# Recurrent layers in blocks of 8 tokens: pair products and block states in place of a scan over all 512 tokens

## The reference

```python
def step(s, rkvw):
    r_t, k_t, v_t, w_t = rkvw
    a = k_t[..., :, None] * v_t[..., None, :]
    out = jnp.einsum('bhi,bhij->bhj', r_t, u * a + s)
    s = a + w_t[..., :, None] * s
    return (s, out)
_, out = jax.lax.scan(step, s0, rkvw)
# then: each head's 16 outputs normalised (mean, variance), * gn_w + gn_b, * g
x1 = x + og * g @ Wo.T
```

## Time and profile before

| | us |
|---|---|
| median of 3 timed runs | 4790.81 (4787.45 to 4797.15) |
| the profiled execution, its own time | 4800.18 |
| its span in the profile | 4798.4 |
| PE busy in the span | 3797.2 (79%) |
| DVE busy in the span | 3378.0 (70%) |
| POOL busy in the span | 2302.9 (48%) |
| ACT busy in the span | 2119.3 (44%) |

### The profile page before, as it was taken

How to read it: one execution, slowest core, us unless ns; L and a number is a source line. 1 busy time by engine, 2 the same in 40 slices (tenths; PEclk the granted TensorE clock), 3 DMA queues, 4 the chain that set the end, 5 groups by cost and what they waited for, 6 DMA issues and landing times. The chain is left out here.

```text
span 4798.4 us, 50379 instructions
## 1 busy us (share of the span) xinstructions
PE 3797.2 (79%) x15616; PEld 2145.1 (45%) x15616; DVE 3378.0 (70%) x5559; ACT 2119.3 (44%) x4624; POOL 2302.9 (48%) x2245
## 2 busy tenths in 40 slices
PE   7888976867888897686788889768668888877766
PEld 4455732424545573252454546234245454623424
DVE  5677379697667738969665773896966577388696
ACT  5576422413657732231365773223137477322313
POOL 4544455354454545535345454543534544454363
PEclk9999977888999998788899999878889999987888
DMA  3123111101212311110121221011022122201102
GB/s 124 39 80 88 53 44 44 44 27 70 70 42 75 88 53 44 49 39 27 70 70 46 74 85 61 36 53 35 27 76 67 49 75 80 77 20 53 35 27 79
DMA packets 95226, 275.38 MB, mean 57 GB/s; under 512 B 25936, under 2 KB 26704, under 8 KB 73808
## 3 DMA queue, kind: packets, MB, share of 16 engines
q1 hardware_dynamic: 94928, 271.84, 17.7%
HBM read 201.49 MB, written 4.19 MB: 43 GB/s over the span
## 5 line engine op out<-in xcount | busy, mean ns | idle before, releaser
L1282 POOL TENSOR_TENSOR prod<-state,rT 128x512 f32<-128x512 f32 x512 | 698.2, 1367 | 662.1 <-DVE state L1060 605.3
L775 POOL TENSOR_SCALAR probs<-probs,row_inv 128x512 f32<-128x512 f32 x1024 | 693.7, 694 | 639.5 <-DVE row_inv L690 639.5
L1060 DVE TENSOR_TENSOR_SCAN state<-decay,s,kvp 128x512 f32<-128x512 f32 x512 | 911.6, 1782 | 12.7 <-POOL prod L1282 12.7
L634 ACT ACTIVATE probs<-probs,row_max 128x512 f32<-128x512 f32 x1024 | 733.3, 725 | 131.2 <-DVE row_max L706 130.0
L529 PE MATMUL ps<-ident,probs 128*128 128x128 f32 x4096 | 605.4, 289 | 172.2 <-ACT pT L628 145.6
L529 PEld LDWEIGHTS ps<-ident,probs 128*128 128x128 f32 x4096 | 476.7, 146 | 382.5 <-ACT pT L628 209.6
L339 PE MATMUL ps<-mix,wring 128*128 128x512 f32 x1024 | 591.6, 677 | 4.8 <-DMA wring<-in_blocks_dram 4.8
L1197 ACT ACTIVATE state<-s 128x1 f32<-128x1 f32 x512 | 102.0, 202 | 1062.2 <-POOL prod L1282 1062.2
L906 PE MATMUL ps<-vstack,pick 128*128 128x512 f32 x512 | 373.7, 732 | 177.0 <-DVE kvp L1052 177.0
L628 ACT ACTIVATE pT<-ps 128x512 f32<-128x512 f32 x768 | 429.8, 603 | 107.8 <-PE ps L529 107.2
L504 PE MATMUL ps<-kstack,qstack 96*128 96x512 f32 (+1 forms) x1024 | 381.6, 467 | 16.8 <-DMA qstack<-hi 7.0
(11 more groups left out here) (142 smaller groups left out, 6526.2 us busy)
## 6 DMA issues: line engine op xcount, KB each, us to landing
wring<-in_blocks_dram SPq DMA_DIRECT2D x151, 1024.0 KB, 5.0
qstack<-hi SPq DMA_DIRECT2D x256, 64.0 KB, 2.0
kstack<-hi SPq DMA_DIRECT2D x256, 64.0 KB, 2.0
maskA<-in_mask_dram SPq DMA_DIRECT2D x9, 1024.0 KB, 7.5
rows<-in_rows_dram SPq DMA_DIRECT2D x8, 1024.0 KB, 4.5
qstack<-hi SPq DMA_DIRECT2D x256, 32.0 KB, 2.0
qstack<-lo SPq DMA_DIRECT2D x128, 64.0 KB, 2.0
kstack<-lo SPq DMA_DIRECT2D x128, 64.0 KB, 2.0
```

The lines of the kernel that those rows point to most:

```text
L634: nc.scalar.activation(p, p, ACT.Exp, bias=row_max[:, n % PSLOTS, qc:qc + 1], scale=-1.0, accum_out=row_sum[:, n % PSLOTS, qc:qc + 1]).the ...
L775: nc.gpsimd.tensor_scalar(p, p, row_inv[:, (n - 1) % PSLOTS, qc:qc + 1], 1.0, ALU.mult, ALU.mult)\
L1060: nc.vector.tensor_tensor_scan(state[:, u % 3, 1:L + 1], decay[:, ug, :], kvp[:, u % 3, :], s0[:, ug, uj:uj + 1], ALU.mult, ALU.add)\
L1282: nc.gpsimd.tensor_tensor(prod[:, t % PRODS, :], state[:, t % 3, 0:L], rT[:, hg % 2, :], ALU.mult)\
```

## The change

The recurrence over 512 tokens is replaced by blocks of 8. What a token receives from tokens of its own block is built from products of pairs, doubled in distance: same token (`rk0`, with u), 1 apart (`rk1`), then the second half of 4 from its first half (`rk2`) and the second half of 8 from its first (`rk4`); k and r are multiplied in place by the decays that lie between. `pair_sums` sums each product per head on PE, DVE multiplies by v (`bonus`), and PE adds it, centred per head, into bank 7 (`bonus_low`, `bonus_high`). What comes from earlier blocks goes through states: `fresh_state` multiplies each block's keys by its values (64 matmuls on 32 x 32 tiles of the array), DVE runs 16 scans over the 64 blocks (`states`), the states are spread to block-diagonal form, four heads by ACT and four by DVE (`spread`), and `from_state` multiplies them by r (2 x 32 matmuls on 128 x 32 tiles). The result is turned into bank 7 (`tokens_to_y`). The variance per head is a matmul with `head_mean`, and POOL raises all 128 x 512 values to -0.5 (`inverse_root`). Wo runs chunk by chunk of features, two chunks of it ahead of the last variance. In each head group the keys are turned to token-major (`keys_to_tokens`) ahead of the next group's key projection (`middle(hg, 0)`).

The diff, cut to its core:

```diff
+            def values_to_tokens(hg):
...
+                for tc in range(C):
+                    m = nc.tensor.matmul(tile[:, tc * P:(tc + 1) * P], vT[:, hg % 2, tc * P:(tc + 1) * P], centre[:, :],
...
+            def pair_sums(hg, level):
...
+                bank, src = ((0, rk0[:, :]), (1, rk1[:, :]), (2, rk2[:, :, :, :]))[level]
+                nc.tensor.matmul(ps[:, bank, 0:256 if level == 1 else 512], head_sum[:, :], src, start=True, stop=True)\
...
+            def pair_sums4(hg):
...
+                for part in range(2):
+                    nc.tensor.matmul(take(pe, 'sums4', l, hg, part), head_sum[:, :], rk4[:, 2 * part:2 * part + 2, :, :],
+                                     start=True, stop=True).then_inc(*tile_ready.reach('sums4', l, hg, part))
...
+            def bonus_low(hg):
...
+                nc.tensor.matmul(y_bank, centre[:, :], rk0[:, :], start=True, stop=False, skip_group_check=True)
+                nc.tensor.matmul(y_bank.rearrange('p (b two) -> p b two', two=2)[:, :, 1], centre[:, :], rk1[:, :],
+                                 start=False, stop=False, skip_group_check=True)
...
+            def bonus_high(hg):
...
+                    m = nc.tensor.matmul(by8[:, :, 1, :], centre[:, :], rk4[:, s, :, :], start=False, stop=False,
...
+            def keys_to_tokens(hg):
...
+                    m = nc.tensor.transpose(tile[:, tc * P:(tc + 1) * P], kT[:, hg % 2, tc * P:(tc + 1) * P], ident[:, :])
...
+            def fresh_state(hg):
...
+                for tc in range(C):
+                    for r in range(4):
+                        rows_ = slice(32 * r, 32 * r + 32)
+                        for q in range(4):
+                            out = ps[32 * q:32 * q + 32, r, :].rearrange('p (two t x) -> p two t x', two=2, t=C)[:, :, tc, :]
+                            m = nc.tensor.matmul(out, k_tok[rows_, tc, 32 * q:32 * q + 32],
+                                                 v_blocks[rows_, tc, q, :, :, :].rearrange('p two b j -> p two (b j)'),
+                                                 start=True, stop=True)
...
+            def from_state(hg, half, tile):
...
+                for tc in (2 * half, 2 * half + 1):
+                    for b4 in range(4):
+                        for q in range(4):
+                            g32 = 4 * tc + q
+                            m = nc.tensor.matmul(tile[32 * q:32 * q + 32, tc * P:(tc + 1) * P],
+                                                 r_blocks[:, 512 * b4 + 32 * g32:512 * b4 + 32 * g32 + 32],
+                                                 state_bd[:, 4 * g32 + b4 - NB // 2 * half, :],
+                                                 start=(b4 == 0), stop=(b4 == 3), skip_group_check=True)
...
-            def reduce(group):
...
-            def centring(c):
-
-                pe.wait_ge(*act_done.when('rec', l, c))
...
-            for t in range(C * HS + lag):
...
-                    nc.tensor.matmul(ps[:, t % 4, :], pick[:, jh * P:(jh + 1) * P], vstack[:, hg % 2, half, :],
-                                     start=True, stop=True)\
...
-            centring(C - 1)
-
-            def wait(pe, c, t):
-                if c == 0:
-                    pe.wait_ge(*dve_done.when('gn', l, t))
-            pe_turn(pe, l, centred, 'gnT', wait)
...
+                    m = nc.tensor.matmul(y_bank[:, tc * P:(tc + 1) * P], y_tok[:, tc, :], ident[:, :], start=False,
...
+                nc.tensor.matmul(take(pe, 'var', l, hg), head_mean[:, :], sqT[:, :], start=True, stop=True)\
...
+            def middle(hg, n):
+                if hg + 1 < C:
+                    project(hg + 1, 'krv'[n])
+                else:
+                    gate(n)
+
+            for hg in range(C):
+                values_to_tokens(hg)
+                pair_sums(hg, 0)
+                pair_sums(hg, 1)
+                if hg > 0:
+                    tokens_to_y(hg - 1)
+                pair_sums(hg, 2)
+                keys_to_tokens(hg)
+                middle(hg, 0)
+                if hg > 0:
+                    variance(hg - 1)
+                fresh_state(hg)
+                pair_sums4(hg)
+                bonus_low(hg)
+                middle(hg, 1)
+                bonus_high(hg)
+                tile = from_state(hg, 0, None)
+                middle(hg, 2)
+                from_state(hg, 1, tile)
+            wo(0)
+            tokens_to_y(C - 1)
+            wo(1)
+            variance(C - 1)
+            gate(C - 1)
+            wo(2)
+            wo(3)
...
+            def pair_products(hg):
...
+                nc.vector.scalar_tensor_tensor(rk0[:, :], r, col(f'u_{l}', hg), k, ALU.mult, ALU.mult)\
...
+                times(rk1[:, :], r1[:, :, 1, 0], k1[:, :, 0, 0], 'rk', l, hg, 1)
...
+                times(k1[:, :, 0, 0], k1[:, :, 0, 0], w[:, :, 1, 0], 'k2', l, hg)
+                times(r1[:, :, 1, 0], r1[:, :, 1, 0], w[:, :, 0, 0], 'r2', l, hg)
...
+                times(rk2[:, :, :, :], r2[:, :, 1, :].unsqueeze(1).to_broadcast(wide),
+                      k2[:, :, 0, :].rearrange('p b s -> p s b').unsqueeze(3).to_broadcast(wide), 'rk', l, hg, 2)
...
+                times(rk4[:, :, :, :], r4[:, :, 1, :].unsqueeze(1).to_broadcast(wide),
+                      k4[:, :, 0, :].rearrange('p b s -> p s b').unsqueeze(3).to_broadcast(wide), 'rk', l, hg, 4)
...
+                times(k4[:, :, 0, :], k4[:, :, 0, :], w[:, :, 1].unsqueeze(2).to_broadcast(wide), 'k8', l, hg)
...
+                times(in_blocks(4), r.rearrange('p (g b t) -> p b g t', b=4, t=8)[:, :, :, 4:8],
...
+                    nc.vector.tensor_tensor(rk4[:, two, :, :], i0, i1, ALU.mult)\
...
+                    ins = nc.vector.scalar_tensor_tensor(
+                        fresh[:, 16 * tc:16 * tc + 16, :].rearrange('p (r b) j -> p r (b j)', r=4), ps[:, 0:4, cut],
+                        masks[:, 12:13], other[:, :, cut], ALU.mult, ALU.add)
...
+                for j in range(HS):
+                    ins = nc.vector.tensor_tensor_scan(entry[:, 1:NB, j], w8[:, hg, 0:NB - 1], fresh[:, 0:NB - 1, j],
+                                                       s0c[:, hg, j:j + 1], ALU.mult, ALU.add)
...
+            def spread(hg, half):
...
+                for h in range(HEADS // 2, HEADS):
+                    ins = nc.vector.tensor_scalar(state_bd[:, :, HS * h:HS * (h + 1)],
+                                                  entry[:, NB // 2 * half:NB // 2 * (half + 1), :], masks[:, 4 + h:5 + h], None,
+                                                  ALU.mult)
...
+            def variance_out(hg):
+                dve.wait_ge(*tile_ready.when('var', l, hg))
+                nc.vector.tensor_scalar(rstdT[:, :], ps[:, ring.bank('var', l, hg), :], 1e-5, None, ALU.add)\
...
+            def normalise(hg):
+                dve.wait_ge(*pool_done.when('rstdT', l, hg))
+                nc.vector.scalar_tensor_tensor(yn[:, hg, :], yT[:, :], col(f'gn_w_{l}', hg), rstdT[:, :], ALU.mult, ALU.mult)\
...
-            for t in range(n + 1):
...
-                    nc.vector.tensor_tensor(kvp[:, t % 3, :], kT[:, hg % 2, :], ps[:, t % 4, :], ALU.mult)\
...
-                    nc.vector.tensor_tensor_scan(state[:, u % 3, 1:L + 1], decay[:, ug, :], kvp[:, u % 3, :],
...
+            for hg in range(C):
+                pair_products(hg)
+                for level in range(3):
+                    bonus(hg, level)
+                if hg > 0:
+                    variance_out(hg - 1)
+                bonus(hg, 4)
+                states(hg)
+                spread(hg, 0)
+                if hg > 0:
+                    normalise(hg - 1)
+                if hg == C - 1:
+                    gated(0)
+                spread(hg, 1)
...
+            low_part('gated', 0, 2)
+            gated(1)
+            gated(2)
+            low_part('gated', 1, 2)
+            low_part('gated', 2, 2)
+            variance_out(C - 1)
+            normalise(C - 1)
+            gated(C - 1)
+            low_part('gated', C - 1, 2)
...
+                nc.scalar.activation(y_tok[:, :, :], ps[:, ring.bank('yt', l, hg), :], ACT.Copy)\
...
+                nc.scalar.activation(sqT[:, :], ps[:, OBANK, :], ACT.Square).then_inc(*act_done.reach('sqT', l, hg))
+                nc.scalar.activation(yT[:, :], ps[:, OBANK, :], ACT.Copy).then_inc(*act_done.reach('yT', l, hg))
...
+                for b4 in range(4):
+                    out = v_blocks[:, :, :, :, b4, :].rearrange('p t q two j -> p (t q two) j')
+                    ins = nc.scalar.activation(out, ps[:, ring.bank('vt', l, hg), :].rearrange('p (x j) -> p x j', j=HS),
+                                               ACT.Identity, scale=masks[:, b4:b4 + 1])
...
+            for hg in range(C):
+                if hg > 0:
+                    y_tokens(hg - 1)
+                value_blocks(hg)
...
+                nc.scalar.activation(in_blocks(0), rT[:, hg % 2, :].rearrange('p (g b t) -> p b g t', b=4, t=8)[:, :, :, 0:4],
...
+                if hg > 0:
```

(39 more changed lines are left out.)

516 lines of the change are left out of this document (265 added, 251 removed).

## The result

| | median of the runs | ratio to before |
|---|---|---|
| before | 4793.98 us (4787.45 to 4810.35, 4 runs) | 1 |
| changed | 6794.94 us (6789.43 to 6797.91, 4 runs) | 1.4165, 95% interval 1.4128 to 1.4203 |
| forecast | 4555 us, range 4400 to 4880 | 0.950 |

A forecast was written before the change was run, and what follows sets the result against it. DVE was taken to bound the recurrent passes before, PE after. Groups 133 plus tail 35.6 make 168.6 us against 198 a pass; eight passes save 235 from 4800.2, giving 4565, timed median 4555; range 4400 to 4880.

The forecast's parts named there:

- What bounds the kernel before: Recurrent scans: DVE decides, busy 158.13 of 160 us, against PE's 110.14.
- I take 8 us, six times the product, as an estimate: Tail of a pass: POOL raises 512 values to -0.5 in 8 us.
- The bounds of 1.4 and 100 us: POOL's power of 512 values: 1.4 us if like a product, 100 us at 0.2 us an element.
- the right rival: POOL's power (p us) is long: slower than before beyond p = 15.1 us, 4950 us at p = 20; chance 0.15.
- That rival's formula: Long power keeping DVE out: excess over 7.6 us counts in three groups, over 8 in the tail; 4p - 31.
- The group, 32.7 us: One head group: PE's 28.1 us at clock 0.9 gives 31.2, with 1.5 of waits 32.7.
- The small tiles: Small matmuls on PE: four run side by side, 0.0275 us an instruction, 7.0 us a group.
- the rival of tiles alone: All small matmuls run one by one at 0.11 us: 21.2 us more a group, 5310 us; chance 0.05.
- `from_state`, which uses all rows, would go one by one: Middle-way rival on PE: only these 128 instructions run alone, 14.1 us for 3.5, kernel 4930 us; chance 0.05.
- The scan of 63 at 0.33: DVE's sixteen scans of 63 elements in a group: 0.33 us each, 5.3 together.
- The lock of 4.5 us: Tail: POOL's weight split after `inverse_root` and a DVE instruction keep each other out, adding 4.5 us.
- The keys' order "at nothing": Turn of keys ahead of the projection, which hides ACT's copy: costs nothing; without that cover 0.8 us a group.

The follow-up runs named there:

- e2_half: Changed kernel with POOL's power on half of the columns and a product on the other half, whose root is left out: 5509.92 us.
- e1_product: Changed kernel with POOL's power replaced by a product of the same operands, the root left out: 4475.85 us.
- g3_alone: Changed kernel with ScalarE square root and VectorE reciprocal for the power, plus `fresh_state` reordered to use each array square four times running: 4812.54 us.
- h1_first_behind: Changed kernel with ScalarE square root, VectorE reciprocal and weight splits in quarters, plus keys turned behind the projection in group 0 alone: 4425.78 us.

## Why the prediction was wrong, point by point

**What bounds the kernel before**: right. DVE's 158 of 160 us did go, and without the power the kernel is 7% faster.

**The step that failed is the tail's term "I take 8 us, six times the product, as an estimate"** for POOL's power of 512 values. It is 82.15 us. The bounds of 1.4 and 100 us held it, and their upper end had been worked out from the only row of the same kind, by 0.2 us an element; e2_half shows 0.16. I chose near the row of the same size and another operation. The two bounds lay a factor of 70 apart (1.4 and 100) and the break-even at 15.1, yet my chance for a power beyond it was about 0.1, and the range ended at 4880, where p is about 18. The text named the right rival, gave its price and its point of decision, and then did not believe it.

**That rival's formula** (what is over 7.6 us counts in three groups, what is over 8 in the tail) gives at 82.15 us 297.8 a pass more, 4555 + 8 x 297.8 = 6937; measured 6795. The waits measured 71.3, 71.3, 71.3 and 82.25. So some 11 us were hidden in a group, not 7.6. Its condition that the power keeps DVE out failed: the scans' median is 0.326 us beside the power and 0.325 without it (e1_product). For the time that decided little: had the scans and the first spreads (5.7 us on DVE) stood behind the power too, it would have cost up to that much in each of 24 groups, some 136 us beside the 2001, an estimate.

**The group, 32.7 us**: 29.2 measured wherever the power is gone. PE's sum of 28.1 at full clock was 27.38 (small tiles 5.8 in place of 7.0, as the sixteen squares of `fresh_state` overlap: 1.9 for its 128), and the clock was 1.00 where I took 0.9, which alone is 3.1 us. The wait of PE for the spread was 1.8, forecast 1 to 1.5. That PE ends last in a group was right.

**The small tiles**: the earlier trace rows were the right guide, and the rival of tiles alone fell; g3_alone comes about half of the way to it by another loop order, 0.060 us each at full clock where the rival had 0.11. That `from_state`, which uses all rows, would go one by one fell too: 64 in 1.95 us, 0.03 each, near the 0.0275 that had four of them side by side.

**The scan of 63 at 0.33**: 0.326 in duration, but 0.25 from start to start. A spread was set at 0.565 and stands at 0.42. So DVE is busy 18.5 us a group, forecast 21.2.

**The lock of 4.5 us**: right in the tail (4.97 beside the split). Missed was the first split, which meets DVE in the last group (4.98 at 988.94). It was not in the sum: in e1_product PE waits 3.41 us there, against 1.82 in the group before. From the power's end to the last normalised tile it was 17.8 us, forecast 4.5 + 2.8 + 1.0 + 8.9 = 17.2.

**The keys' order "at nothing"**: wrong in group 0, where the turn waits for DVE with the projection behind it; h1_first_behind puts 12 us on that for the whole kernel. The 0.8 us without the cover was 0.83.

With 1.3 us for the power the sum of the prediction would have been 4555 - 8 x 6.7 = 4501, against 4476 for e1_product: all other errors together come to 25 us, that of the one term to about 2300. That the 25 is so small is in part luck, since errors cancel in it. The two passes of sample 0 take 154.3 and 156.5 us there (first product to last normalised tile), against 168.6 - 6.7 = 161.9, which alone is some 50 us over eight passes. The tail is as forecast, 29.0 against 28.9; the groups were set too long. If the other samples are alike, the rest lies outside the passes, where the forecast put nothing; no run places it.

## What to carry to other kernels

Where the trace of before has no row for an operation at its new size, the row of the same operation at another size bounds it better than the row of another operation at the same size; and a term with bounds that far apart, on the path, decides the forecast and deserves the chance that its bounds give it. A long instruction off the busiest engine becomes the bound of everything queued behind its reader; ask what stands behind that reader before asking what it hides. Cut long GpSimd instructions with two inputs into pieces where VectorE has short ones to run beside them, and let small tiles of TensorE's array take turns over its squares: a repeated square costs its own time and, in g3_alone, the clock of the matmuls behind it.
